# Two 64-column matmuls or one of 128 columns in the second sweep of a graph network's adjacency products

## The reference, cut to what matters

```python
h = relu(layernorm(x))
T1 = adj @ h
T2 = 2 * (adj @ T1) - h
T3 = 2 * (adj @ T2) - T1
x = x + h @ W[0] + T1 @ W[1] + T2 @ W[2] + T3 @ W[3] + bias0
p = expmap(relu(layernorm(x)))       # row norms, tanh
s = adj @ p
x = x + logmap(s) @ kernel + bias1   # row norms, arctanh
```

## Time and profile before

| | before |
|---|---|
| median of 3 runs | 1873.28 us (1872.55 to 1874.7) |
| profiled execution | 1874.16 us, span 1872.3 us |
| TensorE busy | 1831.8 us (98%), 9600 MATMUL and 9600 LDWEIGHTS records |
| VectorE, ScalarE, GpSimd busy | 433.3, 115.1, 25.4 us |
| moved by DMA | 662.30 MB, mean 354 GB/s |
| mean granted TensorE clock | 0.996 of full |

### The profile page before, as it was taken

One profiled execution on the slowest core, in us unless ns is written; L12 is line 12 of the kernel. 1 busy time (PEld: TensorE's weight loads), 2 busy tenths in 40 slices (PEclk: granted clock), 3 DMA queues, 4 the chain that ended last, 5 costly groups with the idle time before them and its releaser, 6 DMA issues.

```text
span 1872.3 us, 22325 instructions
## 1 busy us (share of the span) xinstructions
PE 1831.8 (98%) x9600; PEld 789.0 (42%) x9600; DVE 433.3 (23%) x886; ACT 115.1 (6%) x208; POOL 25.4 (1%) x39
## 2 busy tenths in 40 slices
PE   6999999999999999999999999999999999999996
PEld 1454444444444444444444444343433333333343
DVE  7322111111112123100000001542322222122147
ACT  0000000000000000000000000311000000000014
POOL 1000000000000000000000000000000000000000
PEclk9999999999999999999999999999999999999998
DMA  9999999999999985888888785799999999999994
GB/s 382 421 421 421 396 401 384 393 389 394 391 386 368 378 329 208 319 294 303 299 294 302 266 303 205 312 379 377 374 379 395 388 379 383 401 387 379 408 403 156
DMA packets 94112, 662.30 MB, mean 354 GB/s; under 512 B 11328, under 2 KB 13376, under 8 KB 13888
## 3 DMA queue, kind: packets, MB, share of 16 engines
q1 hardware_dynamic: 92448, 658.55, 90.5%
q10 hardware_dynamic: 1568, 2.33, 0.3%
HBM read 658.74 MB, written 2.10 MB: 353 GB/s over the span
## 4 chain that ended last, share of the span: by engine, by line
PE 95%; DVE 2%; DMA 1%; issue 1%; ACTq 1%; ACT 0%; DVEq 0%
PE row_bank L482 37%; PE work_bank L462 19%; PE work_bank L496 16%; PE row_bank L451 12%; PE row_bank L484 3%; PE own_bank L510 3%; PE work_bank L464 3%; PE turned L564 2%; DMA ring<-adj_blocks 1%; PE work_bank L533 0%; PE work_bank L521 0%; DVE nodes L870 0%; DVE partial L724 0%; ACTq L578 0%; PE own_bank L564 0%
## 5 line engine op out<-in xcount | busy, mean ns | idle before, releaser
L482 PE MATMUL row_bank<-ring,nodes 128*64 128x512 f32 x1728 | 756.4, 592 | 0.0
L484 PE MATMUL row_bank<-ring,nodes 128*64 128x512 f32 x1728 | 756.4, 592 | 0.0
L482 PEld LDWEIGHTS row_bank<-ring,nodes 128*64 128x64 f32 x1728 | 236.4, 137 | 442.1 <-issue 439.2
L464 PE MATMUL work_bank<-ring,nodes 128*64 128x512 f32 x936 | 420.8, 592 | 0.0
L462 PE MATMUL work_bank<-ring,nodes 128*64 128x512 f32 x936 | 420.8, 592 | 0.0
L496 PE MATMUL work_bank<-ring,nodes 128*64 128x512 f32 x1456 | 343.3, 595 | 0.0
L451 PE MATMUL row_bank<-ring,nodes 128*64 128x512 f32 x1112 | 270.9, 601 | 19.3 <-DVE nodes L677 14.5
L484 PEld LDWEIGHTS row_bank<-ring,nodes 128*64 128x64 f32 x1728 | 236.4, 137 | 0.0
L462 PEld LDWEIGHTS work_bank<-ring,nodes 128*64 128x64 f32 x936 | 127.8, 137 | 216.1 <-issue 216.1
L496 PEld LDWEIGHTS work_bank<-ring,nodes 128*64 128x64 f32 x1456 | 121.4, 138 | 172.4 <-issue 171.4
L724 DVE TENSOR_TENSOR partial<-partial,work_bank 128x512 f32<-128x512 f32 x148 | 101.6, 688 | 326.8 <-PE work_bank L496 326.0
(11 more groups left out here) (98 smaller groups left out, 503.6 us busy)
## 6 DMA issues: line engine op xcount, KB each, us to landing
ring<-adj_blocks SPq DMA_DIRECT2D x626, 1024.0 KB, 7.6
resid<-x ACTq DMA_DIRECT2D x4, 512.0 KB, 11.7
out<-resid SPq DMA_DIRECT2D x16, 128.0 KB, 1.8
w_raw<-cheb_weight ACTq DMA_DIRECT2D x2, 64.0 KB, 28.6
bias<-cheb_bias ACTq DMA_DIRECT2D x1, 32.0 KB, 19.4
bias<-hyp_bias ACTq DMA_DIRECT2D x1, 32.0 KB, 21.4
w_raw<-hyp_kernel ACTq DMA_DIRECT2D x2, 16.0 KB, 29.4
```

What stands on the lines that cost most here:

```text
L464: done = nc.tensor.matmul(bank[EVEN, :], nodes[:, c * C + k, B, :], data[:, k, :], start=k == 0, stop=k == C - 1)
L482: nc.tensor.matmul(bank[ODD, :], nodes[:, c * C + k, A, :], data[:, k, :], start=first and k == 0, stop=last and k == C - 1)
L484: done = nc.tensor.matmul(bank[EVEN, :], nodes[:, c * C + k, B, :], data[:, k, :], start=first and k == 0, stop=last and k == C - 1)
```

## The change

In the second sweep (`level == 2`) the two matmuls of a chunk become one: its stationary operand is both levels of the chunk, 128 columns that lie side by side in `nodes`, and its output the whole bank, all 128 partitions. What is computed, the order of visits, the waits and the semaphore counts stay. The third sweep keeps its pairs, though the same lines issue them.

```diff
                     for k in range(C):
-                        nc.tensor.matmul(bank[ODD, :], nodes[:, c * C + k, A, :], data[:, k, :],
-                                         start=first and k == 0, stop=last and k == C - 1)
-                        done = nc.tensor.matmul(bank[EVEN, :], nodes[:, c * C + k, B, :], data[:, k, :],
-                                                start=first and k == 0, stop=last and k == C - 1)
+                        group = {"start": first and k == 0, "stop": last and k == C - 1}
+                        if level == 2:
+                            done = nc.tensor.matmul(bank[:, :], nodes[:, c * C + k, :, :].rearrange("p l f -> p (l f)"),
+                                                    data[:, k, :], **group)
+                        else:
+                            nc.tensor.matmul(bank[ODD, :], nodes[:, c * C + k, A, :], data[:, k, :], **group)
+                            done = nc.tensor.matmul(bank[EVEN, :], nodes[:, c * C + k, B, :], data[:, k, :], **group)
                     done.then_inc(s_visit, 1)
```

## The result

The changed kernel takes 1878.21 us (median of 11 runs, 1876.57 to 1879.74) against 1873.28 us before (11 runs), a ratio of 1.0025 with a 95% interval from 1.0017 to 1.0034: 4.9 us slower. The profiled span grew by 4.6 us, from 1872.3 to 1876.9 us.

What follows compares the result with a forecast made beforehand. TensorE's matmul stream, busy 98% of the span, was taken as the bound. Slots 0, loads 0 and edges +1.6 us on the 1873.28 us median gave 1874.9, say 1875.0 us; range 1872.0 to 1883.5 us.

Steps and rivals of the forecast that it cites:

- What bounds the kernel, no wait to remove, slots paid for moving columns: Second sweep: TensorE never waits; 912 slots of 0.429 us stay, paid by 512 moving columns, so no change in slot time.
- The load is hidden at 128 columns: Second sweep's runs: full-width weight load, at most 274 ns, stays inside the slot under the running matmul, adding 0 us.
- the rival's sums: Full-width loads not hidden in the second sweep's 912 slots: 55 to 201 us more, about 1930 to 2075 us; chance 9%.
- The term for the edges: At 26 width changes around 13 runs, load not made ahead but stream not emptied: +1.6 us.
- the "same": Whole kernel: no measurable change, less than about 0.2% (3.7 us) from the time before; chance 50%.
- The first rival: Array empties at each of 26 width changes, loads uncovered: 5.7 to 9.9 us more, 1879 to 1883 us; chance 36%.
- The text's lower price: Emptying at 26 edges with 0.16 us tails and short uncovered loads, without the whole recorded load in front: 5.7 us.
- The sign of being wrong: At the second sweep's width changes, a price above 0.14 us an edge would make the forecast wrong.
- The other signs: Second sweep: full-width to TURN start 0.43 us, TURN to run start 0.87 + 0.12 or less, stretch 415 to 417 us.
- The slip of the clock: Between 1178 and 1186 us, reduced clock after TensorE idles takes up to 1.7 us; may come or go with schedule shifts.

## Why the prediction was right, and where not

- *What bounds the kernel, no wait to remove, slots paid for moving columns*: right. The slot is 0.429 us at 32, 64, 96 and 128 columns.
- *The load is hidden at 128 columns*: right; it takes 190 ns, starts with the running matmul and ends in its slot. The rule of the Trainium skill, TensorE: Matmul & The Clock Gate (part 3, the mechanism), is that loads overlap running matmuls only when the row group differs; it doesn't hold here. By the rival's sums, loads without that cover would have cost 55 to 201 us; in the trace the 128-column load of the next matmul runs under one that fills all rows and all columns. That rival is gone.
- *The term for the edges*: the forecast's mechanism (a load not made ahead, the stream not emptied, 1.6 us) was wrong: the load is indeed not made ahead, but TensorE also stops, and the load costs more than the term had. Wrong with it was the "same" as the likeliest. The first rival, to which I gave 36%, came: TensorE stops at each change, and the next load is not made ahead. The text's lower price for it was 5.7 us, and it is 4.5. Two parts of that sum were off against each other. The emptying costs 0.094 us, not the 0.16 us by which a matmul's record outlasts its slot: the next load starts 0.07 us before that recorded end. And the uncovered load costs 0.05 us (64 columns) and 0.105 us (128), not the 0.03 and 0.06 read from the earlier trace rows: those show only from a load's start to its matmul's, and the cost is met one record later, by the second load that stands behind the first.
- The range (1872.0 to 1883.5 us) held 1878.21, because it reached over the rival; the forecast's own mechanism didn't bring it there. The distance from the forecast is 3.2 us. The sign of being wrong that I had given, an edge above 0.14 us on average, is met: 0.175 us. The other signs fell between their marks: from the last full-width start to the TURN's first 0.52 us (0.43 by the forecast, 0.6 or more by the emptying), from the TURN's first start to the run's first 1.02 us (0.99 or 1.1). The stretch grew to 419.5 us, not 415 to 417.
- *The rule of the Trainium skill, TensorEngine Tiling (tiling modes, key properties)*, that changing the mode drains the engine and changing the tile doesn't: the trace agrees in both halves. The changed kernel's edges stop for 0.094 us, and those before, which change only tile and bank, cost nothing.
- *The slip of the clock*: it is in both traces, after the same waits of TensorE early in the third sweep, between 1178 and 1186 us before and some 4 us later in the changed kernel (clock 0.50 from 1184 to 1187 us), and took no part in the difference between these two traces.

## What to carry to other kernels

Two 64-column matmuls in the two halves of the array take one slot together, so merging them to 128 columns saves instructions and no time; on a TensorE-bound kernel the number to count is the changes between array divisions, not the matmuls. Keep one division for as long a run as possible, or give the small matmuls in between the same width; where TensorE waits for another engine soon after, the change is partly free. Read the price of an uncovered load at the second record after a stop, not at the first.

## What the runs showed of the hardware that was not expected

A load right behind a change starts 0.092 us after the stream's end and its matmul 2 ns later: the load itself isn't what the first matmul waits for. Loads of one width into the same columns follow each other at 0.055 us for 64 columns, 0.08 for 96 and 0.108 to 0.112 for 128 (the expectations for short moving operands had 0.053 and 0.106), and two 64-column loads into different halves go side by side. Behind an edge the two halves of a pair start 7 ns apart in place of 36 and stay so, without any gain, since a slot's length is the stream of either.
